# A second product buffer for the first sequence, its successor's norm one pass ahead, an own buffer for totals of decays, and new orders of steps in a token-mixing layer

## What is computed

```python
xn = _ln(x, ln1_w, ln1_b)
sx = _token_shift(xn, state[:, i1])
xxx = jnp.tanh((xn + sx * maa_x) @ maa_w1).reshape(b, l, 5, 1, EXTRA_MAA)
xxx = jnp.matmul(xxx, maa_w2).reshape(b, l, 5, E)
x5 = xn[:, :, None] + sx[:, :, None] * (maa_stack + xxx)
w = jnp.exp(-jnp.exp(time_decay + jnp.tanh(x5[:, :, 1] @ decay_w1) @ decay_w2))
r, k, v = x5[:, :, 3] @ Wr.T, x5[:, :, 0] @ Wk.T, x5[:, :, 2] @ Wv.T
g = jax.nn.silu(x5[:, :, 4] @ Wg.T)
def step(s, rkvw):                        # per head of 16 channels, over the tokens
    a = k_t[:, :, :, None] * v_t[:, :, None, :]
    out = jnp.einsum('bhk,bhkd->bhd', r_t, u * a + s)
    return (a + w_t[:, :, :, None] * s, out)
att = groupnorm(outs) * gn_w + gn_b
x = x + att * g @ Wo.T
xn2 = _ln(x, ln2_w, ln2_b); sx2 = _token_shift(xn2, state[:, i0])
rr = jax.nn.sigmoid((xn2 + sx2 * ffn_maa_r) @ ffn_Wr.T)
kk = jnp.square(jax.nn.relu((xn2 + sx2 * ffn_maa_k) @ ffn_Wk.T))
x = x + rr * (kk @ ffn_Wv.T)
```

## Time and profile before

| | us |
|---|---|
| median of 3 runs | 771.14 |
| lowest to highest | 769.87 to 771.64 |
| span of the profiled execution | 768.0 |
| PE busy | 691.9 |
| VectorE busy | 509.0 |
| GpSimd busy | 388.9 |
| ACT busy | 326.8 |

### The profile page before, as it was taken

How to read it: one execution, slowest core, us unless ns; L and a number is a source line. 1 busy time by engine, 2 the same in 40 slices (tenths; PEclk the granted TensorE clock), 3 DMA queues, 4 the chain that set the end, 5 groups by cost and what they waited for, 6 DMA issues and landing times.

```text
span 768.0 us, 17247 instructions
## 1 busy us (share of the span) xinstructions
PE 691.9 (90%) x7260; PEld 480.3 (63%) x7260; DVE 509.0 (66%) x771; ACT 326.8 (43%) x639; POOL 388.9 (51%) x223
## 2 busy tenths in 40 slices
PE   5895699998999999998999989998899989998577
PEld 4772477657775676756766577746767557755343
DVE  5739744696575865578565967578566858589641
ACT  2240653327441475325733276325733176405411
POOL 1148056565456654575555654565655656364100
PEclk9998989999999989999999999999999999999779
DMA  7900000002000110002000020002000020000000
GB/s 208 393 2 28 9 3 0 1 2 91 2 1 1 34 57 3 3 1 90 3 0 1 2 90 2 1 1 76 17 2 1 1 63 3 27 2 1 30 0 27
DMA packets 13130, 24.57 MB, mean 32 GB/s; under 512 B 3840, under 2 KB 5632, under 8 KB 12032
## 3 DMA queue, kind: packets, MB, share of 16 engines
q1 hardware_dynamic: 13056, 23.47, 8.9%
HBM read 18.35 MB, written 4.19 MB: 29 GB/s over the span
## 4 chain that ended last, share of the span: by engine, by line
PE 79%; ACT 8%; DVE 7%; issue 4%; POOL 1%; DMA 1%; POOLq 0%; SPq 0%; DVEq 0%; ACTq 0%
PE FB L578 26%; PE BAB L838 8%; PE FA L856 7%; PE FB L586 7%; PE FA L879 7%; PE BAB L751 4%; PE FA L656 4%; ACT wide L1017 2%; PE FB L621 2%; PE BAB L781 2%; ACT half L1072 2%; PE BAB L815 2%; PE BAB L569 2%; PE BAB L795 1%; PE FA L569 1%
## 5 line engine op out<-in xcount | busy, mean ns | idle before, releaser
L455 POOL TENSOR_TENSOR mixes<-mixes 128x1024 f32<-128x1024 f32 x30 | 78.7, 2623 | 133.9 <-ACT mixes L991 133.9
L493 POOL TENSOR_TENSOR pp<-rT,kT 128x2048 f32<-128x2048 f32 (+1 forms) x32 | 108.9, 3405 | 54.9 <-DVE rT L1256 51.4
L457 POOL TENSOR_TENSOR mixes<-mixes,xnT 128x1024 f32<-128x1024 f32 x30 | 74.5, 2483 | 2.4
L1351 DVE TENSOR_REDUCE half<-half 128x256 f32<-128x2048 f32 (+2 forms) x32 | 64.5, 2016 | 0.4
L578 PE MATMUL FB<-mixes,wg_s 128*128 128x256 f32 x256 | 62.5, 394 | 0.0
L578 PE MATMUL FB<-mixes,wv_s 128*128 128x256 f32 x256 | 62.3, 395 | 0.1
L578 PEld LDWEIGHTS FB<-mixes,wg_s 128*128 128x128 f32 x256 | 48.0, 194 | 22.5 <-issue 15.1
L856 PE MATMUL FA<-wide,fk_s 128*128 128x256 f32 x256 | 58.3, 387 | 2.2 <-DVE wide L1515 2.2
L578 PE MATMUL FB<-mixes,wk_s 128*128 128x256 f32 x256 | 59.7, 391 | 0.1
L1335 DVE TENSOR_TENSOR half<-BAB,vp 128x2048 f32<-128x2048 f32 x24 | 55.0, 2291 | 6.6 <-PE BAB L751 5.2
L586 PE MATMUL FB<-fr_s,wide 128*128 128x512 f32 x128 | 58.4, 599 | 0.0
(11 more groups left out here) (159 smaller groups left out, 1313.5 us busy)
## 6 DMA issues: line engine op xcount, KB each, us to landing
pp<-x SPq DMA_DIRECT2D x8, 512.0 KB, 4.3
xt<-x SPq DMA_DIRECT2D x8, 512.0 KB, 3.7
out<-wide SPq DMA_DIRECT2D x7, 512.0 KB, 2.9
half<-wv SPq DMA_DIRECT2D x1, 1024.0 KB, 4.7
wk_s<-wk SPq DMA_DIRECT2D x1, 1024.0 KB, 7.1
wr_s<-wr SPq DMA_DIRECT2D x1, 1024.0 KB, 8.2
wg_s<-wg SPq DMA_DIRECT2D x1, 1024.0 KB, 10.2
wo_s<-wo SPq DMA_DIRECT2D x1, 1024.0 KB, 13.6
```

What stands on the lines that cost most here:

```text
L455: nc.gpsimd.tensor_tensor(slot, slot, sx, ALU.mult).then_inc(s_["mixm_ready"], 1)
L457: nc.gpsimd.tensor_tensor(slot, slot, xnT[:, :, 1:L + 1], ALU.add).then_inc(s_["mix_ready"], 1)
L493: ins = nc.gpsimd.tensor_tensor(pp[:, i % 2, 0:size].rearrange("p (n i j) -> p n i j", i=m, j=m), spread(r.unsqueeze(3), 3, m), spread(k.u ...
L1351: nc.vector.tensor_reduce(to, src, AX.X, ALU.add).then_inc(s_["qs_ready"], 1)
```

## The change

- `tot` and `ktok` become two halves of one buffer `tk`; `b_mul1` and `b_mul3` of sequence 0 write there instead of `product` (`product_of`). The waits for `qs_ready` are set to match, and ACT's copy into `ktok` waits for the third reduction of sequence 0.
- Totals of decays get a buffer of their own, `totals_s`; the wait of `b_step1` for the second norm's transposes goes.
- The norm of sequence 1 is transposed, shifted and mixed for the inner tanh in pass `first` (`n_turn`, `n_sx`, `n_xin`) instead of in `second`; its `f_lora` goes into PSUM tensor `FA`, so the waits for the gate go.
- The v transposes of sequence 0 (`f_vtok`) move from `second` to the end of `first`, and `b_score0` waits for their copies.
- On SP the `turn` of sequence 1 comes before the load of sequence 2.
- The lists in `ORDER` change. In `main`, VectorE's `n_norm` moves from ahead of `b_norm2` to the end, `b_step2` ahead of `b_mul0`; PE's `c_fr0` and `b_g0` go ahead of `b_score1` and `c_fv0` behind it, `f_k3` and `f_m23` between `b_apply1` and `b_apply2`, `f_r2` ahead of the second norm's transposes.

The core of the diff (a rename of a helper on SP and equal lists wrapped anew left out):

```diff
     tensor=dict(
         first="""
-            f_norm warm6 f_lora1 f_lora0 f_pair1 f_m20 f_k0 f_k1 f_k2 f_k3 f_dec1 f_pair3 f_dec2 f_v0 f_v1 f_v2
-            f_v3 f_r0 f_r1 f_r2 f_r3""".split(),
+            f_norm warm6 f_lora1 f_pair1 f_lora0 f_m20 f_k0 f_k2 f_k1 f_pair3 f_dec1 f_k3 f_v0 f_v1 f_v2
+            n_turn f_v3 f_r0 f_r1 f_dec2 f_r2 f_r3 f_vtok""".split(),
         second="""
-            b_g0 b_score0 f_norm b_g1 b_score1 b_score2 b_g2 b_score3 b_score4 b_g3 b_vtok f_lora0 b_ktok b_kv0
-            b_kv1 f_m20 f_lora1 f_dec1 f_m21 f_m22 b_acc b_apply0 b_apply1 f_dec2 b_apply2 f_m23 b_apply3 f_k0
-            f_k1 f_k2 f_v0 f_v1 b_gn0 b_gn1 f_k3 b_wo0 b_wo1 f_m24 f_v2 f_v3 b_norm20 f_r0 f_r1 b_norm21 f_r2
-            f_r3""".split(),
+            b_vtok f_lora0 b_g0 f_lora1 b_g2 b_score0 b_g1 b_score1 b_score2 f_m20 b_g3 b_score3 f_m21
+            f_dec1 b_score4 f_dec2 f_m22 b_ktok b_kv0 b_kv1 f_m23 f_k0 f_k1 f_v0 f_k2 f_k3 b_acc b_apply0
+            b_apply1 f_m24 b_apply2 b_apply3 f_v1 f_v2 f_r0 b_gn0 b_gn1 f_v3 b_wo0 b_wo1 f_r1 b_norm20 f_r2
+            b_norm21 f_r3""".split(),
         main="""
-            c_fk b_score0 c_fr0 c_fv0 b_score1 b_g0 b_score2 f_norm c_fr1 b_score3 b_g1 b_g2 b_score4 b_g3 c_fv1
-            b_ktok f_lora0 f_lora1 b_vtok f_m20 f_m21 b_kv0 f_dec1 b_kv1 f_dec2 b_acc f_m22 f_k0 f_k1 f_k2 f_k3
-            b_apply0 b_apply1 b_apply2 b_apply3 f_v0 f_v1 f_m23 f_v2 b_gn0 b_gn1 f_m24 f_v3 b_wo0 b_wo1 f_r0
-            f_r1 b_norm20 b_norm21 f_r2 f_r3""".split(),
+            c_fk c_fr0 b_score0 b_g0 b_score1 c_fv0 b_score2 c_fr1 f_norm b_score3 b_g1 b_g2 b_score4 b_g3
+            c_fv1 f_lora0 b_ktok f_lora1 b_vtok f_m20 f_m21 b_kv0 f_dec1 b_kv1 f_dec2 b_acc f_m22 f_k0 f_k2
+            f_k1 b_apply0 b_apply1 f_k3 f_m23 b_apply2 b_apply3 f_v0 f_v1 f_v2 f_v3 b_gn0 b_gn1 f_r0 f_m24
+            b_wo0 b_wo1 f_r1 f_r2 b_norm20 b_norm21 f_r3""".split(),
         end="""
-            c_fk b_score0 c_fr0 b_score1 f_norm c_fr1 b_score2 b_g0 b_g1 b_g2 b_score3 c_fv0 b_g3 c_fv1 f_lora0
-            b_score4 f_lora1 f_m20 b_vtok f_dec1 b_ktok f_m21 b_kv0 b_kv1 f_dec2 b_acc f_m22 f_k0 f_k1 b_apply0
-            f_k2 f_m23 b_apply1 b_apply2 b_apply3 f_v0 f_m24 f_v1 f_k3 f_r0 b_gn0 b_gn1 f_r1 b_wo0 b_wo1 f_v2
-            f_v3 b_norm20 b_norm21 f_r2 f_r3""".split(),
+            c_fk b_score0 c_fr0 b_score1 f_norm c_fr1 b_score2 b_g0 b_g1 b_g2 b_score3 c_fv0 b_g3 c_fv1
+            f_lora0 b_score4 f_lora1 f_m20 b_vtok f_dec1 b_ktok f_m21 b_kv0 b_kv1 f_dec2 b_acc f_m22 f_k0
+            f_k1 f_m23 b_apply0 f_k2 b_apply1 b_apply2 b_apply3 f_v0 f_m24 f_v1 f_k3 f_r0 b_gn0 b_gn1 f_r1
+            b_wo0 b_wo1 f_v2 f_v3 b_norm20 b_norm21 f_r2 f_r3""".split(),
...
     vector=dict(
         first="""
-            f_xin f_centre f_mix1 f_mix2 f_mix0 n_stats n_norm f_centre0""".split(),
+            f_xin f_centre f_mix1 f_mix2 f_mix0 n_stats n_norm f_centre0 n_xin""".split(),
         second="""
-            b_prodx b_step1 b_mul0 b_step2 b_mul1 b_red1 b_step4 b_gate0 b_mul2 b_red2 b_mul3 b_red3 b_mul4
-            b_step8 b_gate1 f_xin b_red4 f_mix0 b_kv b_scan b_exp b_var0 b_var1 b_root b_nrm0 b_nrm1 n_stats
-            b_gn b_wo0 b_wo1 b_xhat20 b_xhat21 b_norm2 n_norm b_xr""".split(),
+            b_prodx b_step1 b_step2 b_mul0 b_mul1 b_red1 b_step4 b_gate0 b_mul2 f_mix0 b_gate1 b_red2 b_mul3
+            b_step8 n_stats b_mul4 b_red3 b_red4 b_kv b_scan b_exp b_var1 b_var0 b_root b_nrm0 b_nrm1 b_gn
+            b_wo0 b_wo1 b_xhat20 b_xhat21 b_norm2 b_xr n_norm""".split(),
         main="""
-            b_step1 b_mul0 b_step2 c_mul0 b_mul1 b_step4 b_red1 b_mul2 b_red2 b_mul3 b_gate0 b_red3 b_mul4
-            b_step8 f_xin b_gate1 c_mul1 b_red4 f_mix0 n_stats b_kv b_scan b_exp b_var0 b_var1 b_root b_nrm0
-            b_nrm1 b_gn b_wo0 b_wo1 b_xhat20 b_xhat21 n_norm b_norm2 b_xr""".split(),
+            b_step1 b_step2 b_mul0 b_mul1 b_step4 b_red1 c_mul0 b_mul2 b_red2 b_mul3 b_red3 b_mul4 b_step8
+            b_gate0 f_xin c_mul1 b_gate1 b_red4 f_mix0 n_stats b_kv b_scan b_exp b_var0 b_var1 b_root b_nrm0
+            b_nrm1 b_gn b_wo0 b_wo1 b_xhat20 b_xhat21 b_norm2 b_xr n_norm""".split(),
         end="""
-            b_step1 b_mul0 b_step2 b_mul1 b_red1 b_step4 b_mul2 b_red2 b_mul3 b_gate0 f_xin b_step8 c_mul0
-            b_red3 c_mul1 b_gate1 b_mul4 f_mix0 b_red4 b_kv b_scan b_exp b_var0 b_var1 b_root b_nrm0 b_nrm1 b_gn
-            b_wo0 b_wo1 b_xhat20 b_xhat21 b_norm2 b_xr""".split(),
+            b_step1 b_mul0 b_step2 b_mul1 b_red1 b_step4 b_mul2 b_red2 b_mul3 b_gate0 b_step8 f_xin c_mul0
+            b_red3 c_mul1 b_gate1 b_mul4 f_mix0 b_red4 b_kv b_scan b_exp b_var0 b_var1 b_root b_nrm0 b_nrm1
+            b_gn b_wo0 b_wo1 b_xhat20 b_xhat21 b_norm2 b_xr""".split(),
...
     gpsimd=dict(
         first="""
-            n_stats f_mix3 f_sx f_mix4""".split(),
+            n_stats f_mix3 f_mix4 f_sx n_sx""".split(),
         second="""
-            b_prod0 b_prod1 b_prod2 b_prod3 b_add1 b_prod4 b_add2 f_sx b_s0 b_add3 b_add4 f_mix1 f_mix2 f_mix3
-            b_wo0 b_wo1 f_mix4 n_stats""".split(),
+            b_prod1 b_prod2 b_prod3 b_prod4 b_s0 b_add1 b_add2 b_add3 f_mix1 f_mix2 b_add4 b_prod0 f_mix3
+            b_wo0 n_stats b_wo1 f_mix4""".split(),
         main="""
-            b_prod0 b_prod1 b_prod2 b_prod3 b_add1 b_prod4 c_out0 f_sx c_out1 b_s0 b_add2 b_add3 b_add4 f_mix1
-            f_mix2 f_mix3 f_mix4 b_wo0 n_stats b_wo1""".split(),
+            b_prod0 b_prod1 b_prod2 b_prod3 b_prod4 c_out0 b_s0 b_add1 f_sx b_add2 c_out1 b_add3 b_add4
+            f_mix1 f_mix2 f_mix3 f_mix4 b_wo0 n_stats b_wo1""".split(),
         end="""
-            b_prod0 b_prod1 b_prod2 b_prod3 b_prod4 f_sx c_out0 b_add1 b_add2 c_out1 b_s0 b_add3 b_add4 f_mix1
-            f_mix2 f_mix3 f_mix4 b_wo0 b_wo1""".split(),
+            b_prod0 b_prod1 b_prod2 b_prod3 b_prod4 f_sx c_out0 b_add1 b_add2 b_add3 b_s0 c_out1 b_add4
+            f_mix1 f_mix2 f_mix3 f_mix4 b_wo0 b_wo1""".split(),
...
     scalar=dict(
         first="""
-            f_norm f_lora0 f_lora1 f_k0 f_k1 f_dec1 f_mix3 f_mix4 f_v0 f_dec2 f_v1 f_r0 f_r1""".split(),
+            f_norm f_lora1 f_lora0 f_k0 f_dec1 f_mix3 f_k1 f_mix4 f_v0 n_turn f_v1 f_r0 f_dec2 f_r1 f_vtok""".split(),
         second="""
-            f_norm b_g0 b_rcopy b_g1 b_vtok b_ktok b_decays f_lora0 b_kv0 b_kv1 f_lora1 f_dec1 f_mix1 b_exp
-            f_mix2 f_dec2 b_sq0 b_sq1 f_k0 b_gn f_mix3 f_k1 f_mix4 f_v0 f_v1 b_norm2 f_r0 f_r1""".split(),
+            b_g0 f_lora1 f_lora0 b_g1 f_mix1 f_dec1 f_dec2 b_ktok f_mix2 b_decays b_kv1 b_kv0 f_k0 b_vtok
+            f_mix3 b_rcopy b_exp b_sq0 b_sq1 f_k1 f_v0 f_mix4 b_gn f_v1 f_r0 b_norm2 f_r1""".split(),
         main="""
-            c_fk0 c_fk1 c_fr0 c_fr1 f_norm b_rcopy b_g0 b_decays b_g1 b_ktok f_lora0 f_lora1 b_vtok f_mix1 b_kv0
-            f_dec1 b_kv1 f_dec2 f_mix2 f_k0 b_exp b_sq0 b_sq1 f_k1 f_mix3 b_gn f_v0 f_v1 f_mix4 b_norm2 f_r0
-            f_r1""".split(),
+            c_fk0 c_fk1 c_fr0 f_norm c_fr1 b_g0 b_rcopy b_g1 f_lora0 b_ktok b_decays f_lora1 b_vtok f_mix1
+            b_kv0 f_dec1 b_kv1 f_dec2 f_mix2 b_exp f_k0 f_mix3 b_sq0 b_sq1 f_k1 f_v0 b_gn f_mix4 f_v1 f_r0
+            b_norm2 f_r1""".split(),
...
@@ -176,8 +177,9 @@
         pp = sb("pp", [P, 2, 2048])
         acc = sb("acc", [P, C * L])
         vp = sb("vp", [P, C * L])
-        tot = sb("tot", [P, 1024])
-        ktok = sb("ktok", [P, T, E])
+        tk = sb("tk", [P, 2 * T * E])
+        tot = tk[:, 0:T * E]
+        ktok = tk[:, T * E:2 * T * E].rearrange("p (t e) -> p t e", t=T)
 
         wide = sb("wide", [P, PER * T * E + 2 * C])
         vexp = wide[:, 0:PER * T * E].rearrange("p (q t e) -> p q t e", q=PER, t=T)
@@ -188,13 +190,14 @@
         dsh = sb("dsh", [P, C, NC])
         cm_s = sb("cm_s", [P, PER])
         pm_s = sb("pm_s", [P, 2])
+        totals_s = sb("totals_s", [P, C * L])
         gsum = sb("gsum", [P, T * H])
         gvar = sb("gvar", [P, T * H])
         gve = sb("gve", [P, T * H])
         grs = sb("grs", [P, T * H])
         cen = ktok
         xhat = kvs[:, :, :, :].rearrange("p (t d) c n -> p t (d c n)", t=T)
-        x1 = tot[:, :].rearrange("p (t e) -> p t e", t=T)
+        x1 = tot.rearrange("p (t e) -> p t e", t=T)
         st2 = sb("st2", [P, T, 6])
         mv2 = sb("mv2", [P, T, 2])
         ve2 = sb("ve2", [P, T])
@@ -265,13 +268,17 @@
         def totals(m):
 
             at = sum(C * L // q for q in (2, 4, 8, 16, 32, 64, 128) if q < m)
-            return ktok[:, :, :].rearrange("p t e -> p (t e)")[:, at:at + C * L // m]
+            return totals_s[:, at:at + C * L // m]
 
         def added(i):
 
             return adds[:, 512 * i:512 * i + 512]
 
         product = half[:, 0:2048]
+
+        def product_of(b, i):
+
+            return tk[:, :] if first(b) and i in (1, 3) else product
         ru = half[:, 0:C * L]
         wv_raw = half[:, 2048:4096]
...
@@ -388,8 +398,8 @@
```

(27 more changed lines are left out.)

49 lines of the change are left out of this document (28 added, 21 removed).

## The result

The changed kernel takes 789.12 us, the median of four executions (785.27 to 794.37), beside 770.80 for the kernel before (769.87 to 771.64): 1.0236 times as long, 95% interval 1.0186 to 1.0285, or 18.3 us more. The forecast was 779.8 with a range of 762.0 to 789.0, so the sign was right, the forecast rise less than half of the measured one, and the median lies just outside the range.

The account below looks back on a forecast made before the run. PE, busy for 90% of the span, was taken as the bound. Full passes +12.5, clock -1.7, `first` and `second` -3.0, `end` +0.9: together +8.7, so 776.7 profiled and 779.8 as median; range 762 to 789.

Parts of the forecast that it names:

- `first` and `second`: First two passes: later scores but work moved ahead on PE, `c_fk` at 134.1 to 135.8; -3.0 us, bounds -12 and +2.
- `end`: Pass `end`: the late norm lengthens VectorE's stream before `b_score0`, +1.9; mix 3 fills a wait before `b_apply0`, -1.0.
- clock: First full pass: PE's clock no longer falls behind the wait for the second expanded state; -1.7 us, once.
- wait of `b_score1`: Start of each full pass: PE waits for a score that cost it nothing before; +2.7 us, bounds 0 and 3.5.
- gate norm: Each full pass: mix 3's GpSimd instructions beside `root` make PE wait for the normalised tile; +1.4 us.
- The applies: Each full pass: `f_k3` and mix 3 before `b_apply2` cover the wait for the second expanded state; -1.7 us.
- Buffers: Totals' own buffer: 0. Second product buffer: gain at the transpose lost at ACT's copy, 0 together, bounds -2.3 and 0.
- C: Rival: the new order works as laid out, GpSimd's first products overlapping VectorE's stream; 757.4 us, chance 0.22.
- D: Rival: PE's idle time in `second`'s score stretch is filled, giving ten; full passes lose as in A; 772.8 us, chance 0.09.
- B: Rival: only the start of full passes is held up, `root` slips through at the gate norm; 772.8 us, chance 0.13.
- E: Rival: each new 2.7 us wait in full passes lets the clock fall, 1.7 us five times; 788.5 us, chance 0.14.
- A: The forecast itself: VectorE and GpSimd run one after the other at full-pass start and gate norm; 779.8 us, chance 0.42.

Follow-up runs that it names:

- new_main: The kernel before with the change's four `main` lists (order of the full passes) and nothing else of it: 782.18 us, ratio 1.0150.
- old_main: The changed kernel with the four `main` lists (order of the full passes) of the kernel before: 774.92 us, ratio 1.0039.
- norm_late: The kernel before with `n_norm` at the end of VectorE's `main` list and nothing else: 772.41 us, ratio 1.0018.
- exp_first: The kernel before with ACT's `b_exp` ahead of `f_k0` in the full passes and nothing else: 771.62 us, ratio 0.9986.
- mix3_back: The changed kernel with mix 3 behind v1 on PE and behind `f_k1` on ACT in `main`: 795.95 us, ratio 1.0322.
- score_back: The changed kernel with `b_mul0` ahead of `b_step2` and `c_fv0` ahead of `b_score1` again in the full passes: 791.47 us, ratio 1.0248.
- fill_score: The changed kernel with seven small matmuls on PE between `b_g0` and `b_score1` of each full pass: 792.67 us, ratio 1.0265.
- one_product: The changed kernel with one product buffer for every sequence and `b_red3` ahead of `b_mul4` in `second`: 791.32 us, ratio 1.0270.

## Where the forecast was right and where it failed

Forecast +8.7: order +10.4 (12.5 for the full passes, -3.0 for `first` and `second`, +0.9 for `end`) and clock -1.7. Measured as means of spans, +18.0: order +14.4 and clock +3.6. Of the 9.3 us between them the clock makes 5.3 (standard error 1.3), the order outside the full passes 2.4 (+0.3 instead of -2.1) and the full passes 1.6 (14.1 instead of 12.5).

*Full passes, waits: the sum right, in part by luck.* Forecast +2.5 a pass, +12.5. Measured: `new_main` has a rest of +12.8, and the changed kernel less `old_main` gives 14.4 - 0.3 = 14.1. Single terms were off and cancelled. The wait of `b_score1` is 7.9 / 5 = 1.6 (2.7 forecast), as the keys came 0.7 earlier. That of the gate norm is 1.0 (1.4). `c_fk` starts 0.4 later (0.1). The applies gave back 3.5 / 5 = 0.7 (1.7). I had read one pass whose wait on the second state was 1.7; over five passes it had been 8.1 us, and 4.6 remain. The waits sum to +11.5; the next term would make up what is missing to 14.1.

*Full passes, PE's own work: missed.* In the pass of the earlier trace rows at a granted clock of 1.00 PE is busy for 82.78 us; the like pass of `new_main`, with the same matmuls, shows 83.72 (its window):

```profile
410.87:501.28 90.41, 83.72 (x904) 57.28 (x905) 66.40 (x93) 41.02 (x82) 49.43 (x28) 1.00 0.06 20
```

Over the passes of the changed kernel it is 0.7 more than in those of before with as much time at 1.2 GHz. It is spread over many groups: between the two passes at a granted clock of 1.00 the k tiles take 0.27 us more and the transposes of the gate norm and the second norm 0.27, while the v tiles take 0.54 less. Why is not shown. Five times 0.7 is 3.5 us, which with the 11.5 makes 15.0, near the 14.1.

*The clock: the step that failed first.* I had the clock give back 1.7 us, because one wait ahead of the applies was followed by a fall. That fall is indeed gone: the first full pass of the changed kernel's trace has 3.4 us at 1.2 GHz and that before 6.8. But others came, and there are 27 us at 1.2 GHz in its five full passes, beside 20 before. Over executions the clock's part is not -1.7 but +3.6 us, and it is as large in `old_main` (3.3), whose full passes are the old ones, while in `new_main`, with the new ones, it is -1.7. With the 74.6 and 64.5 us of the two groups of kernels this puts the loss, about 10 us more at 1.2 GHz or 3.3 us of span, on what the ten kernels share: the buffers and the passes outside the full ones, for which I had put the clock at nothing without a reason. In which of them isn't settled, since the time at 1.2 GHz up to the first full pass varies from 20.5 to 37.5 us between executions of the same code (before and `norm_late`).

*`first` and `second`: the other step that failed.* Forecast: `b_mul4` at 84.7, applies done at 109 to 111, `c_fk` at 134.1 to 135.8. VectorE's timeline of the changed kernel:

```profile
71.70 4.25 DVE L1257 TENSOR_TENSOR mixes<-mixes,xnT 128x512 f32<-128x512 f32 x2
...
80.86 2.08 DVE L1276 TENSOR_TENSOR kT<-kT,totals_s 128x512 f32<-128x512 f32 x1
82.86 2.19 DVE L1309 TENSOR_TENSOR dsh<-totals_s 128x60 f32<-128x60 f32 x1
...
87.05 2.26 DVE L1361 TENSOR_TENSOR half<-BAB,vp 128x2048 f32<-128x2048 f32 x1
...
103.82 7.54 DVE L1424 TENSOR_TENSOR wide<-kvs,cm_s 128x1024 f32<-128x1024 f32 x2
...
117.04 1.28 DVE L1489 TENSOR_REDUCE gvar<-wide 128x32 f32<-128x512 f32 x2 [5.67 <-ACT wide L1104]
```

GpSimd beside them:

```profile
80.04 2.35 POOL L465 TENSOR_TENSOR mixes<-mixes 128x1024 f32<-128x1024 f32 x1
82.47 2.50 POOL L467 TENSOR_TENSOR mixes<-mixes,xnT 128x1024 f32<-128x1024 f32 x1
...
103.59 2.36 POOL L465 TENSOR_TENSOR mixes<-mixes 128x1024 f32<-128x1024 f32 x1 [3.58 <-ACT mixes L1010]
106.03 3.67 POOL L467 TENSOR_TENSOR mixes<-mixes,xnT 128x1024 f32<-128x1024 f32 x1
```

The fourth multiplication came 2.35 late against the forecast: step 8 met both of mix 1's instructions, not one, and the copy of 60 elements (L1309), which took 0.22 us in the kernel before, took 2.19: it ended with the GpSimd instruction beside it (85.05 and 84.97). The two instructions of the expansion (L1424) took 7.54 us for what had taken 3.71 there, because the order puts mix 3's two GpSimd instructions beside it: 3.8 more. How much of it reaches `c_fk` is not shown: PE is busy up to the applies, and inside them it waits 1.7 and 1.2 us. The lateness adds up to 6.2, and `c_fk` came at 140.67, 5.7 after the middle of my forecast; the last stretch, 25 us from the applies to `c_fk`, was as I had it. I had walked the port meetings up to `b_mul4` and stopped there. These are single executions, and one code reaches its first full pass at different times: 136.18 to 142.02 in the four traces with the old passes (before, `new_main`, `exp_first`, `norm_late`; mean 139.2), and 137.76 to 140.95 in the five with the changed kernel's own (changed, `old_main`, `mix3_back`, `score_back`, `fill_score`; mean 139.5). So the 3.0 us of gain are not there, and over all executions the order outside the full passes is worth +0.3 (`old_main`), where I had -2.1.

*`end`: the sum hardly off, the steps wrong.* `b_score0` followed `c_fk` without a wait, as GpSimd's first two products got in ahead of VectorE's small instructions there too (603.70 and 606.34, done at 608.0), so my +1.9 wasn't there; nor was the -1.0, for the apply there waits 1.8 instead of 1.0. It took 2.1 more.

*Buffers: right.* `one_product` shows no difference for the second product buffer (14.4 beside 14.4, to within 1.5 us), and `old_main` holds it with the totals' buffer and the SP order at +0.3.

*Rivals.* C and D (the score chain works as laid out, `second` gives ten) are out: full passes of 91.8 to 93.9 us, `c_fk` at 140.67. B is out: the gate norm waits in each pass, and ends when mix 3 moves. E gave nearly the right total, 788.5, for the wrong reason, by luck: its falls behind the waits are there twice in five, filling the waits makes the kernel no faster, and the clock's loss is as large in `old_main` without them.

*Sums.* A's own range counts the bound of the gate norm once. Five passes with 0 to 3.6 us instead of 1.4, and `second` with -12 to +2 instead of -3.0, give 764 to 796 and not 771 to 787, and the measured median lies inside that. E is 779.8 and five times 1.7, which is 788.3. A third of the 0.22 of B and D is 0.07 and not 0.09, so "faster" should have had 0.26.

## What to carry to other kernels

Walk an order to the last engine that the chain crosses: in `second` the walk was 2.35 us off at the last meeting of VectorE and GpSimd that was priced, and a meeting behind it, not priced, held the expansion up for another 3.8. A wait taken out of a chain of three engines moves to the next one: three of the edits that undid a part of the change, each aimed at a visible wait, made the kernel slower still. Before the clock is given a term with a sign, look at how much time at 1.2 GHz one and the same code has in several executions, and do not hold one trace against another without their mean clocks beside them.

## What the runs showed of the chip

- One kernel, 45 executions: 44 to 80 us at 1.2 GHz, and spans that follow it with 0.33 us per microsecond. Two profiled executions with the same code up to the first full pass had 20.5 and 37.5 us at 1.2 GHz there, and reached it at 137.92 and 142.02.
- VectorE instructions with next to no work last until the GpSimd instruction that they meet has ended: 0.22 to 2.19 us for 60 elements a partition (L1309), 0.20 to 2.21 for 64 (L1444).
- A stream of small VectorE instructions can let a GpSimd instruction in, and then pays for it: six of L1541 took 5.79 us with two GpSimd products inside. In the kernel before, the same kind of stream held the product for 4.28 us. Both times the product was issued 0.2 us after a VectorE instruction had begun, so an estimate has to allow for both outcomes.
